# A graph convolution on one core: the order of each engine's work within a block is rewritten, and GpSimd waits per chunk

## The chip, the cores and the metric

The kernel runs on one core of a Trainium2 chip. The metric is the device time of one execution in microseconds (us). Three runs were timed, and one further execution was profiled. The engines are called TensorE (PE; PEld is its weight load), VectorE (DVE), ScalarE (ACT), GpSimd (POOL) and SyncE (SP), as in the profile.

## The reference, cut to what matters

12500 nodes with 128 features, 412500 edges sorted by destination. For each edge a small network of its 8 scalars gives 4 x 32 weights, which multiply the source node's features; four attributes enter as well, and the edges' results are summed by destination.

```python
x0, x1 = node_input[:, :32], node_input[:, 32:].reshape(N, 32, 3)
f0 = x0 @ W1_0e / sqrt(32); f1 = einsum('nui,uw->nwi', x1, W1_1o) / sqrt(32)
feat0, self0 = f0[:, :32], f0[:, 32:]; feat1, self1 = f1[:, :32], f1[:, 32:]
e0, e1 = feat0[edge_src], feat1[edge_src]
h = gelu(edge_scalar_attr @ W_mlp1 / sqrt(8)); h = gelu(h @ W_mlp2 / sqrt(64))
w00, w01, w10, w11 = h @ Wp_00, h @ Wp_01, h @ Wp_10, h @ Wp_11
mid0 = [w00*e0*ea0, w11*sum(e1*ea1)/sqrt(3)]; mid1 = [(w01*e0)*ea1, w10*e1*ea0]
n0, n1 = segment_sum(mid0, edge_dst), segment_sum(mid1, edge_dst)
y = cos(MIX)*self + sin(MIX)*(n @ W2)
out = layernorm(x + y)
```

## The kernel before

A prologue multiplies all nodes by their weights, stores the table of features in DRAM, lays the self part into `acc` (feature by node, in SBUF), and turns the sorted indices into `src_all` and `rel_all` (each destination as an offset from its tile's base). Then come 202 blocks of 2048 edges: 16 tiles of 128 edges, in four chunks of four tiles. An epilogue transposes `acc` and normalises rows.

For each block the engines do the following, each in its own list, and they meet only through semaphores:

- POOL (`gather_block`, L448): 16 indirect gathers (`gather`, L434), each 128 rows of 512 B from the table, into one of four slots of `gath`. Ahead of a block it waits for the indices and for `s_prod[3]` of the block four back, whose slot it takes.
- PE: of the hidden layers, `layer1` (L729) and `layer2` (L733) for two halves h of a later block, all four results in one PSUM bank (`hid_ps`), so they alternate with ACT's gelus; `radial` (L737), the product with `wpbd` for a chunk, into that chunk's bank (2 to 5); `segment_sum` (L750), four matmuls of a chunk with the selection, into bank 6; `transpose_sums` (L764), four transposes of a pair of chunks into bank 7; `convolve` (L773), four matmuls into bank 1 (`y_ps`).
- DVE: `select` (L974) makes the selection (offset equals window position, times the edge's attributes); `products` (L1002) multiplies a chunk's radial weights by gathered rows, three instructions (L994, L997 twice); `add_windows` (L1016) adds 16 windows of 8 nodes into `acc` at bases from registers.
- ACT: `gelu1` (L515), `gelu2` (L520), `lay_attributes` (L526), which copies the attributes into PSUM for DVE, `copy_sums` (L534) of bank 6 to `zsb`, `copy_transposed` (L538) of bank 7 to `ztsb`, `copy_indices` (L500) for the block seven ahead.
- SP loads attributes and scalars in a ring of eight blocks.

A block's work ahead of the loop is called `step`; PE's (L781), DVE's (L1025) and ACT's (L546) set the order by hand, as do the loops of eight steps that follow. One bank for the sums means that a pair of chunks must be copied out by ACT before the next pair is summed, so sums of chunks 2 and 3 of block b-1 stand within step b:

```python
segment_sum(b, s, 0, first)
...
layer1(s, 1)
radial(b, s, 3, first)
segment_sum(b, s, 1)
...
layer2(b + SUPER, 1)
transpose_sums(b, 0, first)
```

## Time and profile before

| what | us |
|---|---|
| median of 3 runs | 5393.78 |
| lowest, highest | 5361.47, 5398.54 |
| the profiled execution | 5384.89 |
| its span, first to last instruction | 5383.0 |
| PE busy | 3296.7 (61% of the span) |
| POOL busy | 3103.5 (58%) |
| DVE, ACT busy | 1881.7 (35%), 1178.5 (22%) |
| granted TensorE clock, mean | 0.767 |

The profile is of a single execution. "Idle before" is an engine's idle time just ahead of an instruction, with what ended it; "remote" is written where no releaser was found, "issue" where the engine waited for nothing that the profile shows. The ends of matmuls are modelled. Register, semaphore and DMA-issuing instructions don't count as busy, except POOL's indirect gathers.

### The profile page before, as it was taken

The numbers are of one execution on the slowest core, as the hardware profiler recorded it, in microseconds if no ns is written. First come the engines' busy times: TensorE is split into PE (matmuls) and PEld (weight loads), VectorE is DVE, ScalarE is ACT, GpSimd is POOL, SyncE is SP. The second block draws the span as 40 slices with busy tenths as digits, with TensorE's granted clock in tenths as the row PEclk, the third lists the DMA queues.
The fourth block names the chain that finished last, engine by engine and source line by source line (L and its number), as shares of the span: only waits on it lengthen the run. The fifth ranks groups of instructions, "written<-read, shape, count | busy, mean of one in ns | idle before, by whom it ended". The sixth has DMA issues, their size and how long they took to land.

```text
span 5383.0 us, 53986 instructions
## 1 busy us (share of the span) xinstructions
PE 3296.7 (61%) x15272; PEld 1820.5 (34%) x15272; DVE 1881.7 (35%) x6401; ACT 1178.5 (22%) x2646; POOL 3103.5 (58%) x3281
## 2 busy tenths in 40 slices
PE   6566655666665665666566555666666665666666
PEld 5333333333333333333333333333333333333334
DVE  2333333333333333333333333333333333333335
ACT  3222122222222221222222222222222222222224
POOL 5466555566655565556655665556565566555651
PEclk8777777777777777777777777777777787778777
DMA  6122112212212122222221221212222122122211
GB/s 152 34 47 46 44 42 44 44 44 47 46 43 46 42 46 44 44 45 45 46 45 43 47 46 42 45 44 46 43 46 45 43 46 46 43 46 45 46 45 60
DMA packets 586055, 256.02 MB, mean 48 GB/s; under 512 B 528383, under 2 KB 531867, under 8 KB 584347
## 3 DMA queue, kind: packets, MB, share of 16 engines
q0 software_dynamic: 103616, 211.52, 15.1%
q1 hardware_dynamic: 480572, 42.82, 6.7%
q14 instruction: 160, 1.31, 0.1%
q10 hardware_dynamic: 1696, 0.18, 0.0%
q8 instruction: 11, 0.18, 0.0%
HBM read 241.45 MB, written 12.81 MB: 47 GB/s over the span
## 4 chain that ended last, share of the span: by engine, by line
another core or an unknown queue 51%; PE 27%; issue 13%; ACT 8%; DVE 0%; ACTq 0%; DMA 0%; DVEq 0%; POOL 0%; POOLq 0%
PE bank L735 6%; PE bank L778 5%; PE bank L730 5%; PE bank L745 5%; PE bank L759 3%; PE bank L770 2%; ACT h L517 2%; ACT big L522 1%; ACT ztsb L543 1%; ACT ztsb L544 1%; PE bank L677 1%; ACT bank L532 1%; ACT idx L501 1%; ACT big L635 1%
## 5 line engine op out<-in xcount | busy, mean ns | idle before, releaser
L436 POOL DMA_INDIRECT gath<-feature_table,idx x3224 | 3077.2, 954 | 2149.6 <-issue 1711.0
L745 PE MATMUL bank<-wpbd,big 128*128 128x256 f32 x3232 | 982.4, 433 | 27.1 <-issue 25.5
L994 DVE TENSOR_TENSOR big<-bank,gath 128x256 f32<-128x256 f32 x808 | 342.2, 424 | 1737.2 <-remote 1481.8
L778 PE MATMUL bank<-ztsb,conv 128*128 128x128 f32 x1616 | 360.4, 392 | 865.4 <-ACT ztsb L544 574.8
L745 PEld LDWEIGHTS bank<-wpbd,big 128*128 128x128 f32 x3232 | 707.5, 225 | 472.5 <-issue 404.1
L997 DVE TENSOR_TENSOR big<-bank,gath 128x384 f32<-128x384 f32 x1616 | 817.9, 548 | 0.0
L770 PE MATMUL bank<-ident,zsb 128*128 128x128 f32 x1616 | 342.8, 351 | 700.3 <-issue 505.4
L735 PE MATMUL bank<-h,w2bd 128*128 128x512 f32 x804 | 571.8, 801 | 232.2 <-ACT h L517 128.0
L1022 DVE TENSOR_TENSOR acc<-acc,bank 128x8 f32 x3232 | 528.7, 164 | 509.4 <-PE bank L778 93.3
L730 PE MATMUL bank<-e8T,w1bd 128*128 128x512 f32 x804 | 571.0, 799 | 156.2 <-ACT big L522 77.6
L778 PEld LDWEIGHTS bank<-ztsb,conv 128*128 128x128 f32 x1616 | 308.1, 285 | 982.5 <-issue 492.6
L759 PE MATMUL bank<-big,sel 128*32 128x256 f32 x6464 | 593.4, 444 | 8.8 <-DVE big L997 8.7
L770 PEld LDWEIGHTS bank<-ident,zsb 128*128 128x128 f32 x1616 | 258.4, 183 | 970.1 <-issue 749.1
L522 ACT ACTIVATE big<-bank 128x512 f32<-128x512 f32 x402 | 440.7, 1096 | 618.4 <-PE bank L735 403.5
L536 ACT COPY zsb<-bank 128x512 f32<-128x512 f32 x404 | 237.9, 589 | 1124.4 <-remote 1033.2
L981 DVE TENSOR_TENSOR sel<-rel_all,bank 128x128 f32<-128x128 f32 (+1 forms) x202 | 58.1, 288 | 1102.1 <-issue 940.4
L517 ACT ACTIVATE h<-bank 128x512 f32<-128x512 f32 x402 | 242.1, 602 | 778.7 <-remote 368.0
L543 ACT COPY ztsb<-bank 128x64 f32<-128x64 f32 x404 | 95.8, 237 | 1440.6 <-remote 1364.8
L730 PEld LDWEIGHTS bank<-e8T,w1bd 128*128 128x128 f32 x804 | 145.7, 227 | 380.2 <-issue 235.3
L735 PEld LDWEIGHTS bank<-h,w2bd 128*128 128x128 f32 x804 | 154.0, 238 | 333.3 <-issue 190.7
L759 PEld LDWEIGHTS bank<-big,sel 128*32 128x32 f32 x6464 | 135.7, 115 | 286.2 <-issue 286.1
L986 DVE TENSOR_TENSOR sel<-sel,bank 128x512 f32<-128x512 f32 x202 | 138.7, 686 | 6.9
(83 smaller groups left out, 799.0 us busy)
## 6 DMA issues: line engine op xcount, KB each, us to landing
gath<-feature_table,idx POOLq DMA_INDIRECT x3224
e<-in_edge_attr SPq DMA_DIRECT2D x416, 32.0 KB
ea_t<-in_edge_attr SPq DMA_DIRECT2D x100, 64.0 KB
feature_table<-gath SPq DMA_DIRECT2D x4, 1280.0 KB, 5.6
out<-big SPq DMA_DIRECT2D x4, 1280.0 KB
big<-in_x SPq DMA_DIRECT2D x3, 1280.0 KB, 8.4
dst_rows<-in_dst SPq DMA_DIRECT2D x1, 1536.0 KB
big<-in_src SPq DMA_DIRECT2D x1, 1408.0 KB
```

The source lines that it names most:

```text
L436: pool.indirect_dma_start(out=gath[:, s % SLOTS, t, :], out_offset=None, in_=table[:, :], in_offset=bass.IndirectOffsetOnAxis(ap=idx[:, s, ...
L517: act.activation(h1[:, h, :], hid_ps[:, :], ACT.Gelu_apprx_tanh, scale=1.0 / math.sqrt(RADIAL)).then_inc(s_h1[h], 1)
L522: act.activation(h2[:, m // SUPER % 2, :, :, 2 * (m % SUPER) + h], hid_ps[:, :].rearrange("q (b p) -> q b p", b=SUPER), ACT.Gelu_apprx_tan ...
L730: pe.matmul(hid_ps[:, :], w1bd[:, 2 * (m % SUPER) + h, :], e8T[:, :], start=True, stop=True)\
L735: pe.matmul(hid_ps[:, :], w2bd[:, :], h1[:, h, :], start=True, stop=True).then_inc(s_h2p[h], 1)
L745: last = pe.matmul(wgt_ps[c][:, 256 * r:256 * (r + 1)], h2[:, s // SUPER % 2, s % SUPER, 16 * g:16 * (g + 1), :].rearrange("q p a -> q (p ...
L759: last = pe.matmul(z_ps[32 * t:32 * (t + 1), c % 2, :], sel[:, s % 2, CT * c + t, :, :].rearrange("q k w -> q (k w)"), prod[:, c, t, :], s ...
L770: last = pe.transpose(zt_ps[:, h, c, :], zsb[:, c, 128 * h:128 * (h + 1)], ident[:, :])
L778: last = pe.matmul(y_ps, conv[:, k, :], ztsb[:, k, :], start=(k == 0), stop=(k == 3))
L994: dve.tensor_tensor(o[:, :, :, 0, :], w[:, :, :, 0, :], f[:, :, 0, :].unsqueeze(2).to_broadcast([128, n, 2, MUL]), ALU.mult)
L997: last = dve.tensor_tensor(o[:, :, h, 1:4, :], w[:, :, h, 1, :].unsqueeze(2).to_broadcast([128, n, 3, MUL]), f[:, :, 1:4, :], ALU.mult)
L1022: dve.tensor_tensor(acc[:, at], acc[:, at], y_ps[:, WINDOW * t:WINDOW * (t + 1)], ALU.add)\
```

## The change

The number of matmuls, products, gathers and additions stays. What changes:

- `step` becomes `cycle` on PE, ACT and DVE, in another order. The hidden layers run for block b+5 and b+6 rather than b+4. Radial products of chunks 0 and 1 are made for block b+2, of 2 and 3 for b+1. All four chunk sums of a block stand in a row, and both pairs are transposed in the next cycle.
- Sums and transposes of pair 0 are in bank 6, of pair 1 in bank 7, in turn; `zsb` holds both pairs.
- Products of chunks 0 and 1 of odd blocks go to another buffer (`prod_odd`, in `dst_rows`), so that these chunks' products may be one block further ahead of the sums.
- POOL waits ahead of every chunk for that chunk's product four blocks back (the argument `b_stop` is not used).
- The attributes and the window positions are read from SBUF (`ea_t`, `iota_w`), and `lay_attributes` is gone; SP waits for the selection instead.

```diff
+        prod_odd = dst_rows[:, 0:2 * CT, :].rearrange("q (c t) f -> q c t f", c=2)
+        def prod_at(s, c):
+            return prod_odd[:, c] if c < 2 and s % 2 else prod[:, c]
...
-        z_ps = bank[6][:, :].rearrange("q (c f) -> q c f", c=2)
-        zt_ps = bank[7][:, :].rearrange("q (h c n) -> q h c n", h=2, c=2)
+        z_ps = [bank[6 + i][:, :].rearrange("q (c f) -> q c f", c=2) for i in range(2)]
+        zt_ps = [bank[6 + i][:, :].rearrange("q (h c n) -> q h c n", h=2, c=2) for i in range(2)]
...
-                    if free is not None:
-                        pool.wait_ge(s_prod[CHUNKS - 1], free)
-                        pool.sem_inc(s_round, 1)
                     for c in chunks:
+                        if free is not None:
+                            pool.wait_ge(s_prod[c], free)
+                            pool.sem_inc(s_round, 1)
                         gather(s, c)
...
+            def cycle(b, s, group):
+                k = s + SUPER + 2
+                if s > -2:
+                    gelu1(b + (SUPER + 1), 1)
+                if s > 0:
+                    copy_sums(b - 1, 0)
+                    copy_sums(b - 1, 1)
+                if s > -2:
+                    gelu2(b + (SUPER + 1), k - 1, 1)
+                if k % SUPER == 0:
+                    copy_e8T(group)
+                gelu1(b + (SUPER + 2), 0)
+                if s > 0:
+                    copy_transposed(b - 1, 0)
+                    copy_transposed(b - 1, 1)
+                gelu2(b + (SUPER + 2), k, 0)
+                if s > 0:
+                    act.wait_ge(s_prod[CHUNKS - 1], b + 0)
+                    copy_indices(b + (RING - 1), (s + RING - 1) % RING).then_inc(s_idx, 1)
...
             def segment_sum(b, s, c):
                 if c == 0:
                     pe.wait_ge(s_sel, b + 1)
+                    if s > 0:
+                        pe.wait_ge(s_zt, b * 2)
...
-                dve.wait_ge(s_eap, b + 1)
                 dve.tensor_tensor(sel01[:, :, :], rel_all[:, ts_].unsqueeze(2).to_broadcast([128, TILES, WINDOW]),
-                                  iota_ps.unsqueeze(1).to_broadcast([128, TILES, WINDOW]),
+                                  iota_w[:, :].unsqueeze(1).to_broadcast([128, TILES, WINDOW]),
                                   ALU.is_equal).then_inc(s_sel0, 1)
                 dve.wait_ge(s_sel0, b + 1)
...
-                                  attr.unsqueeze(3).to_broadcast([128, TILES, 4, WINDOW]), ALU.mult).then_inc(s_sel, 1)
+                                  ea_t[:, s % RING, :, :].unsqueeze(3).to_broadcast([128, TILES, 4, WINDOW]),
+                                  ALU.mult).then_inc(s_sel, 1)
...
-                if not first:
-                    dve.wait_ge(s_seg[c], b)
+                if c < 2 and s > 1:
+                    dve.wait_ge(s_seg[c], b - 1)
+                if c >= 2 and s > 0:
+                    dve.wait_ge(s_seg[c], b + 0)
```

The first `cycle` shown is ACT's. PE's and DVE's are best seen in the order of their instructions. In the rows below a bank's number is PSUM's: bank0 the hidden layers, bank1 the convolution, bank2 to bank5 the radial products of chunks 0 to 3, bank6 and bank7 sums and transposes.

PE before, the middle of a step in the loop: from the transposes of the last block's second pair to the convolution.

```order
L770 MATMUL bank7<-ident,zsb 128x128 [waits transposed_sums_copied,sums_copied]
L770 MATMUL bank7<-ident,zsb 128x128 x3
L754 REGISTER_ALU [waits selection_ready]
L759 MATMUL bank6<-big,sel 32x256 [waits products_ready0,sums_copied]
L759 MATMUL bank6<-big,sel 32x256 x3
L730 MATMUL bank0<-e8T,w1bd 128x512 [waits gelu2_done0]
L745 MATMUL bank5<-wpbd,big 128x256 [waits products_ready3]
L745 MATMUL bank5<-wpbd,big 128x256
L759 MATMUL bank6<-big,sel 32x256 [waits products_ready1]
L759 MATMUL bank6<-big,sel 32x256 x3
L776 REGISTER_ALU [waits window_added15,transposed_sums_copied]
L778 MATMUL bank1<-ztsb,conv 128x128 [waits selection_ready]
```

Sums of chunks 0 and 1 stand apart, with first layer and radial 3 between them, and the four transposes wait for sums copied within the step.

PE of the changed kernel, the first part of a cycle: from the first layer of the half 0 to radial 0 and 1 of a later block.

```order
L722 MATMUL bank0<-e8T,w1bd 128x512 [waits gelu2_done1]
L737 MATMUL bank5<-wpbd,big 128x256 [waits products_ready3]
L737 MATMUL bank5<-wpbd,big 128x256
L759 MATMUL bank6<-ident,zsb 128x128 [waits sums_copied]
L759 MATMUL bank6<-ident,zsb 128x128 x3
L759 MATMUL bank7<-ident,zsb 128x128 x4
L727 MATMUL bank0<-h1,w2bd 128x512 [waits gelu1_done0]
L737 MATMUL bank2<-wpbd,big 128x256 [waits products_ready0]
L737 MATMUL bank2<-wpbd,big 128x256
L737 MATMUL bank3<-wpbd,big 128x256 [waits products_ready1]
L737 MATMUL bank3<-wpbd,big 128x256
```

All eight transposes stand in a row behind one wait, early in the cycle, and the two radial products follow at once.

PE of the changed kernel, the rest of that cycle.

```order
L749 MATMUL bank6<-dst_rows,sel 32x256 [waits products_ready0,transposed_sums_copied,selection_ready]
L749 MATMUL bank6<-dst_rows,sel 32x256 x3
L749 MATMUL bank6<-dst_rows,sel 32x256 [waits products_ready1]
L749 MATMUL bank6<-dst_rows,sel 32x256 x3
L749 MATMUL bank7<-big,sel 32x256 [waits products_ready2]
L749 MATMUL bank7<-big,sel 32x256 x3
L749 MATMUL bank7<-big,sel 32x256 [waits products_ready3]
L749 MATMUL bank7<-big,sel 32x256 x3
L766 MATMUL bank1<-ztsb,conv 128x128 [waits window_added15,transposed_sums_copied]
L766 MATMUL bank1<-ztsb,conv 128x128 x3
L722 MATMUL bank0<-e8T,w1bd 128x512 [waits gelu2_done0]
```

The four sums stand together behind one wait for the transposed sums' copies; before, only two stood between such waits. The first layer's second half closes the cycle.

DVE before, one step from chunk 1's product on (`sel01` and `sel` are the selection, `base_row` the load of the bases).

```order
L994 TENSOR_TENSOR big<-bank3,gath 128x8x32 [waits segments_summed1,gathered2_1,radial_weights_done1]
L997 TENSOR_TENSOR big<-bank3,gath 128x4x96 x2
L980 REGISTER_ALU [waits selection_ready,segments_summed3]
L981 ISA [waits attributes_in_psum]
L981 TENSOR_TENSOR sel01<-rel_all,bank1 128x128
L986 TENSOR_TENSOR sel<-sel01,bank1 128x512 [waits onehot_ready]
L994 TENSOR_TENSOR big<-bank4,gath 128x8x32 [waits segments_summed2,gathered2_2,radial_weights_done2]
L997 TENSOR_TENSOR big<-bank4,gath 128x4x96 x2
L1010 ISA
L1010 TENSOR_LOAD base_row
L994 TENSOR_TENSOR big<-bank5,gath 128x8x32 [waits segments_summed3,gathered2_3,radial_weights_done3]
L997 TENSOR_TENSOR big<-bank5,gath 128x4x96 x2
```

DVE of the changed kernel, one cycle from its start: the products of chunks 2 and 3 (into `big`), then 0 and 1 of the next block (here into `dst_rows`), then the bases; the two instructions of the selection and the 16 additions follow.

```order
L978 TENSOR_TENSOR big<-bank4,gath 128x8x32 [waits segments_summed2]
L981 TENSOR_TENSOR big<-bank4,gath 128x4x96 x2
L978 TENSOR_TENSOR big<-bank5,gath 128x8x32 [waits segments_summed3,gathered2_3,radial_weights_done3]
L981 TENSOR_TENSOR big<-bank5,gath 128x4x96 x2
L987 REGISTER_ALU
L978 TENSOR_TENSOR dst_rows<-bank2,gath 128x8x32 [waits segments_summed0,gathered3_0,radial_weights_done0]
L981 TENSOR_TENSOR dst_rows<-bank2,gath 128x4x96 x2
L978 TENSOR_TENSOR dst_rows<-bank3,gath 128x8x32 [waits segments_summed1,gathered3_1,radial_weights_done1]
L981 TENSOR_TENSOR dst_rows<-bank3,gath 128x4x96 x2
L996 ISA
L996 TENSOR_LOAD base_row
L960 ISA
```

Four products now stand in a row; before, the selection and the load of bases stood between them.

## Rows read from the trace of the kernel before

**Rows 1.** The page: DMA queues, then groups of instructions.
```profile
q0 software_dynamic: 103616, 211.52, 15.1%
...
L436 POOL DMA_INDIRECT gath<-feature_table,idx x3224 | 3077.2, 954 | 2149.6 <-issue 1711.0
...
L994 DVE TENSOR_TENSOR big<-bank,gath 128x256 f32<-128x256 f32 x808 | 342.2, 424 | 1737.2 <-remote 1481.8
...
L981 DVE TENSOR_TENSOR sel<-rel_all,bank 128x128 f32<-128x128 f32 (+1 forms) x202 | 58.1, 288 | 1102.1 <-issue 940.4
...
L986 DVE TENSOR_TENSOR sel<-sel,bank 128x512 f32<-128x512 f32 x202 | 138.7, 686 | 6.9
```

**Rows 2.** Groups by line, POOL alone, 240.9 to 5273.2 us.
```profile
L436 POOL DMA_INDIRECT gath<-feature_table,idx x3120 | 2977.8, 954 | 2055.5 <-issue 1617.3 <-DVE big L997 438.3
```

**Rows 3.** POOL's waits in that stretch: total us, times, longest us.
```profile
POOL gath L436 <- DVE big L997: 438.3, 72, 11.6
```

**Rows 4.** Timeline of one block: start us, us, engine, line, operation [idle before].
```profile
2105.28 0.96 POOL L436 DMA_INDIRECT gath<-feature_table,idx  x1 [5.41 <-issue]
...
2109.00 1.13 PE L730 MATMUL bank<-e8T,w1bd 128*128 128x512 f32 x2
...
2109.96 1.03 PE L745 MATMUL bank<-wpbd,big 128*128 128x256 f32 x4
...
2110.84 0.60 ACT L517 ACTIVATE h<-bank 128x512 f32<-128x512 f32 x1 [2.28 <-PE bank L730]
...
2110.92 0.64 PE L759 MATMUL bank<-big,sel 128*32 128x256 f32 x8
...
2112.45 1.03 PE L745 MATMUL bank<-wpbd,big 128*128 128x256 f32 x4
...
2113.72 0.42 DVE L994 TENSOR_TENSOR big<-bank,gath 128x256 f32<-128x256 f32 x1 [2.05 <-remote]
...
2118.69 0.58 ACT L536 COPY zsb<-bank 128x512 f32<-128x512 f32 x1 [7.25 <-remote]
...
2119.33 1.12 PE L770 MATMUL bank<-ident,zsb 128*128 128x128 f32 x4 [5.85 <-issue]
...
2124.17 0.95 POOL L436 DMA_INDIRECT gath<-feature_table,idx  x1 [0.30 <-issue]
...
2125.05 0.42 DVE L994 TENSOR_TENSOR big<-bank,gath 128x256 f32<-128x256 f32 x1 [3.40 <-remote]
...
2127.87 0.21 ACT L543 COPY ztsb<-bank 128x64 f32<-128x64 f32 x1 [7.37 <-remote]
...
2128.07 0.42 DVE L994 TENSOR_TENSOR big<-bank,gath 128x256 f32<-128x256 f32 x1 [1.67 <-remote]
...
2128.19 0.62 ACT L517 ACTIVATE h<-bank 128x512 f32<-128x512 f32 x1
...
2128.41 1.01 DVE L997 TENSOR_TENSOR big<-bank,gath 128x384 f32<-128x384 f32 x2
...
2130.20 0.95 POOL L436 DMA_INDIRECT gath<-feature_table,idx  x1 [5.08 <-issue]
```

**Rows 5.** DVE's group L916: 97 to 151 us (gathers run), 161 to 178 us (none).
```profile
L916 DVE COPY acc<-bank 128x500 f32<-128x500 f32 x6 | 4.1, 679 | 54.7 <-remote 44.2 <-issue 10.5
...
L916 DVE COPY acc<-bank 128x500 f32<-128x500 f32 x7 | 4.8, 679 | 1.9 <-PE bank L690 1.9
```

**Rows 6.** Timeline, POOL: first gather of block 1.
```profile
91.10 0.95 POOL L436 DMA_INDIRECT gath<-feature_table,idx  x1 [0.30 <-issue]
```

**Rows 7.** POOL's gathers of the steady part, by source line.
```profile
L436 POOL DMA_INDIRECT gath<-feature_table,idx x3120: 949/955/972, 240.9 to 5267.4; - x195
```

**Rows 8.** Timeline, POOL: the first gather that waits for products.
```profile
190.03 0.95 POOL L436 DMA_INDIRECT gath<-feature_table,idx  x1 [38.77 <-issue]
```

**Rows 9.** Timeline: the last gather (POOL), the last additions (DVE).
```profile
5282.10 0.95 POOL L436 DMA_INDIRECT gath<-feature_table,idx  x1 [0.30 <-issue]
...
5328.19 4.58 DVE L1022 TENSOR_TENSOR acc<-acc,bank 128x8 f32 x16 [2.28 <-PE bank L778]
```

More of the change, by code:

```diff
@@ new lines, in cycle @@
+            def cycle(b, s, group, round_):
+                i, k = b + (SUPER + 2), s + SUPER + 2
+                if s > -2:
+                    layer2(b + (SUPER + 1), 1)
+                if s > -2:
+                    radial(b + 1, s + 1, 2)
+                if k % SUPER == 0:
+                    transpose_e8(k % RING, round_, i)
+                    pe.wait_ge(s_e8T, group + 1)
+                else:
+                    pe.wait_ge(s_h2[1], i)
+                layer1(k, 0)
+                if s > -2:
+                    radial(b + 1, s + 1, 3)
+                if s > 0:
+                    transpose_sums(b - 1)
+                layer2(i, 0)
+                radial(b + 2, s + 2, 0)
+                radial(b + 2, s + 2, 1)
+                if s >= 0:
+                    for c in range(CHUNKS):
+                        segment_sum(b, s, c)
+                if s > 0:
+                    convolve(b - 1)
+                pe.wait_ge(s_h2[0], b + (SUPER + 3))
+                layer1(k, 1)
@@ L1023, in add_windows, with cycle @@
                         .then_inc(s_add[t], 1)
[L1025 to L1034 removed]
+            def cycle(b, s, n, skipped=0):
+                if s >= 0:
+                    products(b, s, 2, n * 2 + s // SLOTS)
+                    products(b, s, 3, n * 2 + s // SLOTS)
+                if s >= -1:
+                    products(b + 1, s + 1, 0, n * 2 + (s + 1) // SLOTS - skipped)
+                    products(b + 1, s + 1, 1, n * 2 + (s + 1) // SLOTS - skipped)
+                    base = load_bases(b - 2) if s >= 2 else None
+                    select(b + 1, s + 1, (n + (s + 1) // RING) * 16 + 16)
+                if s >= 2:
+                    add_windows(b - 2, base)
             flag = dve.value_load(flag_i[0:1, 0:1], min_val=0, max_val=NODES)
```

208 lines of the change are left out of this document (67 added, 141 removed).

## The prediction

> **What bounds the kernel now.** First the page's DMA queues and groups of costly instructions: the gathers' queue takes 15.1% of the DMA engines' time, GpSimd (POOL) has 3224 gathers to issue, and the other engines' large idle times end with "remote", a releaser that the profile can't name [rows 1]. No engine or queue is full, so the waits must be read in order of time.
>
> POOL's own group in the steady part comes next [rows 2]: 5032.3 us hold 3120 gathers, 195 blocks of 16, so a block takes 25.81 us. A gather is 0.954 us and the next follows 0.30 us later; 16 x 0.954 + 15 x 0.30 = 19.8 us is a burst. The idle 2055.5 us less 195 x 15 x 0.30 leave 1178 us, 6.0 us per block, in which POOL stands still. 19.8 + 6.0 = 25.8: the period is a burst and a stop, and an edit counts only if it changes one of the two. Stops run up to 11.6 us [rows 3].
>
> The timeline shows what a stop is made of [rows 4]. POOL waits for product 3 of the block four back. Look at when that becomes possible. TensorE (PE) ends the sums of chunk 3 (L759) at 2111.56, and ACT, which waits for just that, starts its copy only at 2118.69, 7.1 us later. The transposes end at 2120.45, and the copy that waits for them starts at 2127.87, 7.4 us later. The radial product of chunk 2 ends at 2113.48, and VectorE (DVE) begins on it at 2125.05. DVE doesn't wait for gathered rows there: POOL has issued them three blocks before. At the start of the burst it is not so: the first layer ends at 2110.13 and its gelu starts at 2110.84. After the last gather (ends 2125.12) all that is outstanding is let go: copy 2127.87, product 2128.07, gelu 2128.19. So while POOL issues, a finished matmul is seen late by whoever waits, and it comes out at the latest 2.75 us after the last gather. That this belongs to the gathers the prologue shows: the same copy L916, fed by the same matmuls, idles 54.7 us before 6 copies while POOL gathers, and 1.9 us before 7 when it doesn't [rows 5]. I call the release behind a burst the flush.
>
> Of the Trainium skill, "SBUF — State Buffer", section "SBUF: two separate sides", this speaks against: engine ports and DMA ports can't contend, and PE and ACT never wait on anyone. [Rows 4, 5] show waits on PE that depend on POOL's gathers; the measurement decides, and the sum stands on it.
>
> The stop, step by step [rows 4]: 2.75 us to the flush, 0.2 us to the start of DVE's product (2127.87 to 2128.07), 1.35 us for its three instructions (to 2129.42), 0.78 us to POOL's first gather at 2130.20: 5.08 us. The mean is 6.0, so 0.96 us per block is lateness: blocks in which PE still had a dependent step to do when POOL stopped, here the chain sums 3, copy, transposes, copy, and first layer, gelu, second layer, gelu, first layer, all ahead of radial product 3 in PE's list.
>
> **The change, part by part.**
> POOL's waits. Four waits on a register value per block in place of one, and each is met by a product of its own chunk. The next burst starts at chunk 2 (product 2 of the new VectorE cycle comes first) and runs over c2, c3, c0, c1, since the four products then follow each other at 1.35 us while four gathers take 5.0. I expect again 16 gathers between two stops. Cost of three more waits: nothing to 0.3 us (another issue gap) each in a burst; in the prologue the second block's first gather also stands behind a wait (for its indices), and follows in the usual 0.30 us [rows 6], so I take nothing. The index copy that POOL also waits for stays at the end of ACT's list and runs seven blocks ahead; SP's loads wait for the selection instead of the attribute copy, and load as many blocks ahead as before.
>
> PE's list. No matmul is added or removed. In a cycle PE now does the second layer, radial 2, first layer, radial 3, eight transposes, second layer, radial 0 and 1, four sums, convolution, first layer. The radial products that DVE needs behind the next flush are all done early in the burst. What must be seen within a burst before the sums can run is the first layer (gelu) and the transposes (their copies hold the sums' banks); the long pair sums-copy-transposes has its first half at the flush, where it is free. In [rows 4] the first layer (ends 2110.13, 4.9 us into the burst) is seen 0.7 us later, radial 1 (ends 2110.99, 5.7 us) 2.7 us later, sums 3 (6.3 us) 7.1 us later. The new transposes end about 6 us into the burst: after the flush gelu 0.6, second layer 1.1, gelu 1.1, first layer 1.1, radial 1.0, transposes 1.1 and issue in between make some 8 us, and the burst starts 2.1 us behind the flush. Seen 2.7 to 7.1 us later, copied in 0.5 to 1 us, and followed by four sums at 0.64 us and the loads between them, the sums end 12 to 18 us into a burst of 19.8. So PE mostly has nothing left that DVE needs when POOL stops.
> New stop: 2.75 + 0.3 (sums 0 and 1 and others stand ahead of sums 2 in the release; in [rows 4] copy, product and gelu come out over 0.3 us) + 1.35 + 0.78 = 5.18 us. Of the 0.96 us of lateness I leave 0.36: 5.54 us. Bounds: 5.1, the shown stop, and 11.6, the longest; the value lies between the shown one and today's mean, the rows nearest to it. Gain 0.50 us per block.
>
> The second bank for the sums and the doubled products of chunks 0 and 1 only make this order possible: copies and products are as many and as long as before. ACT's copy of attributes (L532) goes; ACT idles 7.25 and 7.37 us before its two copies [rows 4], so nothing.
>
> DVE's selection. Both instructions, 0.288 and 0.686 us [rows 1], now read two operands from SBUF, where the second used to be in PSUM. They fall into the burst, 5.4 us behind the flush. The trace has no such instruction beside a gather. Bounds: nothing, or POOL held for both, 0.98 us per block; less than nothing is excluded, since POOL doesn't wait for them. DVE itself has the time (idle 1737 us before L994, [rows 1]). I take 0.2 us, nearer to nothing, because gathers keep 949 to 972 ns beside all that DVE does now [rows 7].
> The same page and section of the Trainium skill has a rule here: a DVE instruction with two SBUF inputs and a GpSimd one that reads SBUF lock each other out for the whole instruction. By it the upper bound would hold; it is a rival below.
>
> Ends. The first gather that waits starts at 190.03 [rows 8], behind product 3 of block 0. It will wait for product 0 only, about 5 us earlier. From the last gather's end (5283.05) to the end of the last additions (5332.77) four blocks take 49.7 us, 12.4 each [rows 9]. The additions now come a block later and the hidden layers are two blocks ahead instead of fewer, so about one block more: +12 us. Together +7.
>
> Sum: 198 blocks x (-0.50 + 0.20) = -59, +7: -52 us. From the profiled execution, 5384.9 us (span 5383.0 and 1.9 around it), that is 5333. The median of the three runs is 8.9 above the profiled one, so I forecast 5342 us, 1.0% under 5393.8.
>
> **Rivals.**
> Nothing changes. The flush is what POOL waits for, both lists need one, and 6.0 us remain. For it: the stop shown is already 5.08, within 0.1 of the new floor. Against it: the mean is 0.96 above. 5393.8 + 7 = 5401, "same".
>
> The selection holds POOL (other side). If both instructions stop the gathers, +0.98 in place of +0.20: 198 x 0.78 = +154, so 5496. It decides against the change from 0.5 us per block on. For it: select now falls always into a burst. Against it: no row shows POOL held by DVE.
>
> The sums come too late (other side). They now need the transposes of the same burst to be seen and copied, behind PE's in-order list. If these are seen only at the flush, their copies and four sums at 0.64 us or more follow while POOL stands, and a stop is 5 us longer, like those of up to 11.6 us [rows 3, 4]. Ten more such stops eat up the gain of 52; in 40 of 198 blocks it is +200: 5540.
>
> POOL gets past a chunk. If product 2 is released within the burst, 20 gathers run per stop in place of 16; the stop of 5.5 us is then spread over 1.25 blocks, -1.1 us per block: 5342 - 218 = 5124. Against it: eleven results stand ahead of sums 2, and [rows 4] show one release in 5 to 6 us there (2113.72, 2118.69, 2125.05).
>
> **Chances and range.** Forecast case (stop 5.2 to 5.8, selection up to 0.4) 0.50, between 5240 and 5400: 0.32 of it faster, 0.18 same. Nothing changes 0.12. Selection holds POOL 0.13 (0.09 slower, 0.04 same). Late sums 0.15 (0.13 slower, 0.02 same). Past a chunk 0.10. Faster by over 1% 0.42, within 1% 0.36, slower by over 1% 0.22; 1% is about what a measurement of this kernel tells from no change (its three runs lie 0.7% apart). Lower end: stop at its floor of 5.18 and selection free give 198 x -0.86 + 7 = -163, so 5230. Upper end: 5496, the selection's price. I give 5230 to 5500.
>
> **What would show it.** POOL's group: idle per block (now 6.0 beside the 4.5 of issue gaps) should fall to 5.5, with bursts still 16 gathers, beginning at chunk 2. A gather of 1.2 us and more, or gaps over 0.30 beside the selection rows, would show the lock. If ACT's copies of transposes or PE's sums appear in the stops, the list is late. If bursts of 20 or no stops appear, the delay isn't what I take it for and the forecast is far too high; two stops per block would put it at 30 us a block.

## The result, and the profile after

The changed kernel takes 5424.75 us (median of 17 runs, 5416.69 to 5431.13) beside 5392.95 us of the kernel before (17 runs). The ratio on record is 1.0054, with a 95% interval from 1.0036 to 1.0071. It is slower by 0.5%: within the 1% that the prediction called "same" and inside its 5230 to 5500 us, but on the other side of no change from the 1.0% faster that it gave as its number. The profiled execution has a span of 5429.1 us, 46.1 more than before; the medians differ by 32.

The first view is POOL again, in the same stretch as [rows 2, 3]: its group, then its waits (total us, times, longest us).

```profile
L439 POOL DMA_INDIRECT gath<-feature_table,idx x3098 | 2959.9, 955 | 2072.6 <-DVE big L981 1170.9 <-issue 901.7
```

```profile
POOL gath L439 <- DVE big L981: 1170.9, 194, 9.0
POOL gath L439 <- issue: 901.7, 2904, 0.9
```

A gather is as long as before. The pattern stands as forecast: 194 stops with 16 gathers between two of them, all behind DVE's product, and nothing but issue gaps elsewhere. 1170.9 / 194 is 6.04 us per stop, where 5.5 were forecast. Before it was 5.88: the 195 stops of [rows 2], counted one by one in the timeline, sum to 1146.9 us. (The prediction's 6.0 came from taking 0.30 us for every issue gap; they are 0.311 on the mean, before and after.) The longest stop is 9.0 us in place of 11.6. So the stops were not shortened; their mean grew by 0.16 us.

The mean hides the cause. POOL's idle times before the first gather of each burst, read one by one over the two traces and sorted by whether ACT copied fresh scalars (`e8T`) in that block, give this table. Every fourth block has such a copy, because the scalars of four blocks are transposed together.

| mean stop, us | before | after |
|---|---|---|
| 49 blocks with a copy of `e8T` | 6.80 | 7.88 |
| 146 other blocks | 5.57 | 5.41 |
| stops under 5.4, of 196 | 74 | 100 |
| stops of 6.5 and more, of 196 | 22 | 57, 48 of them with `e8T` |

49 x 1.08 - 146 x 0.16 = +30 us. Three blocks in four gained 0.16 us each, the fourth gave it back and more. These blocks were already the longer ones before, by 1.2 us; now it is 2.5. What those blocks wait for has rows of its own. First the groups of the kernel before, in the stretch of [rows 2]: PE's transposes of the scalars and ACT's copy of them.

```profile
L699 PE MATMUL bank<-ident,e 128*128 128x128 f32 x196 | 31.8, 288 | 0.0
...
L513 ACT COPY e8T<-bank 128x512 f32<-128x512 f32 x49 | 28.7, 585 | 87.8 <-PE bank L699 54.6 <-issue 33.3
```

The same two groups of the changed kernel:

```profile
L691 PE MATMUL bank<-ident,e 128*128 128x128 f32 x196 | 53.3, 427 | 363.3 <-DMA e<-in_edge_attr 301.7 <-issue 61.6
...
L516 ACT COPY e8T<-bank 128x512 f32<-128x512 f32 x49 | 28.7, 586 | 412.8 <-PE bank L691 270.6 <-issue 142.2
```

PE never waited for scalars before. Now it stands still for them 363.3 us, 7.4 per time, and what ends most of the wait is the transfer of the scalars (`e`). Their transposes began 3.2 us into a burst on the mean before, and 11.8 now (10.8 to 13.6 in the 49 blocks). The timeline of one such block shows what follows (start us, us, engine, line, operation):

```profile
2640.58 0.95 POOL L439 DMA_INDIRECT gath<-feature_table,idx  x1 [5.22 <-DVE big L981]
...
2642.88 1.07 ACT L532 COPY zsb<-bank 128x512 f32<-128x512 f32 x2
...
2643.10 0.95 POOL L439 DMA_INDIRECT gath<-feature_table,idx  x1 [0.30 <-issue]
...
2643.81 0.69 DVE L969 TENSOR_TENSOR sel<-sel,ea_t 128x512 f32<-128x512 f32 x1
...
2644.36 0.97 POOL L439 DMA_INDIRECT gath<-feature_table,idx  x1 [0.30 <-issue]
2644.68 0.39 SPq L345 DMA_DIRECT2D ea_t<-in_edge_attr  x1
2645.25 6.36 SPq L316 DMA_DIRECT2D e<-in_edge_attr  x4
...
2651.60 1.09 PE L691 MATMUL bank<-ident,e 128*128 128x128 f32 x4 [6.58 <-DMA e<-in_edge_attr]
...
2652.73 0.59 ACT L516 COPY e8T<-bank 128x512 f32<-128x512 f32 x1 [7.44 <-PE bank L691]
...
2653.37 2.07 PE L722 MATMUL bank<-e8T,w1bd 128*128 128x512 f32 x2 [0.68 <-issue]
...
2656.94 1.91 PE L759 MATMUL bank<-ident,zsb 128*128 128x128 f32 x8
...
2659.48 0.96 POOL L439 DMA_INDIRECT gath<-feature_table,idx  x1 [0.30 <-issue]
...
2662.14 0.21 ACT L539 COPY ztsb<-bank 128x64 f32<-128x64 f32 x1 [6.07 <-remote]
...
2663.58 0.21 ACT L539 COPY ztsb<-bank 128x64 f32<-128x64 f32 x1 [1.00 <-remote]
...
2664.07 1.93 PE L749 MATMUL bank<-big,sel 128*32 128x256 f32 x32 [2.59 <-ACT ztsb L540]
...
2665.74 0.42 DVE L978 TENSOR_TENSOR big<-bank,gath 128x256 f32<-128x256 f32 x1 [16.39 <-PE bank L749]
...
2667.87 0.95 POOL L439 DMA_INDIRECT gath<-feature_table,idx  x1 [7.43 <-DVE big L981]
```

Read it from the selection (2643.81) on. As soon as it ends, SP issues a load of attributes and then four of scalars, in the order of its list. PE has been standing at the transposes of just those scalars. They arrive at 2651.60, 11 us into the burst, and behind them in PE's list stand the first layer, a radial product and the eight transposes of sums. These end at 2658.85, their copies start only at 2662.14, when POOL has stopped, and the sums run in the stop. That is a stop of 7.43 us. The first gather that waits for products, and the last gather, hold the rest of the 46.1 us:

```profile
187.68 0.96 POOL L439 DMA_INDIRECT gath<-feature_table,idx  x1 [36.66 <-issue]
...
5312.33 0.96 POOL L439 DMA_INDIRECT gath<-feature_table,idx  x1 [0.30 <-issue]
```

From the last gather's end to the end of the span are 115.8 us; before they were 100.0 (from [rows 9] and the span). The first gather that waits starts 2.35 us earlier (187.68 for 190.03 in [rows 8]). -2.35 + 15.8, and +32.6 between these two points, are the 46.1; the +30 of the stops is nearly all of the 32.6.

### The profile page after: what moved, and what is told of

It reads as the page before. It is cut to its first block, busy times and chain, and to the rows that moved or that the text cites. A ratio compares the mean times of both kernels' runs of the same rounds, so it can differ in the third digit from the quotient of the medians.

```text
span 5429.1 us, 53623 instructions
## 1 busy us (share of the span) xinstructions
PE 3437.7 (63%) x15318; PEld 1905.2 (35%) x15318; DVE 1813.9 (33%) x6409; ACT 1173.1 (22%) x2455; POOL 3106.7 (57%) x3281
## 4 chain that ended last, share of the span: by engine, by line
issue 64%; PE 11%; SPq 10%; another core or an unknown queue 8%; DVE 4%; ACT 2%; DVEq 1%; DMA 0%; ACTq 0%; POOL 0%; POOLq 0%
SPq L316 8%; PE bank L749 3%; PE bank L722 2%; PE bank L737 2%; PE bank L727 1%; PE bank L766 1%; DVE big L981 1%; DVE acc L1008 1%; SPq L345 1%; PE bank L669 1%; ACT big L627 1%; DVE dst_rows L981 1%; SPq L366 1%; PE bank L759 0%
## 5 line engine op out<-in xcount | busy, mean ns | idle before, releaser
L749 PE MATMUL bank<-big,sel 128*32 128x256 f32 x4848 | 834.3, 509 | 1029.4 <-issue 830.0
L978 DVE TENSOR_TENSOR big<-bank,gath 128x256 f32<-128x256 f32 x608 | 252.9, 416 | 3040.6 <-remote 1811.2
L737 PE MATMUL bank<-wpbd,big 128*128 128x256 f32 x3256 | 867.2, 402 | 0.0
L749 PEld LDWEIGHTS bank<-big,sel 128*32 128x32 f32 x4848 | 251.0, 131 | 1524.4 <-issue 1286.8
L981 DVE TENSOR_TENSOR big<-bank,gath 128x384 f32<-128x384 f32 x1216 | 613.9, 545 | 0.0
L727 PE MATMUL bank<-h,w2bd 128*128 128x512 f32 x814 | 464.8, 654 | 142.6 <-ACT h L520 139.1
L691 PE MATMUL bank<-ident,e 128*128 128x128 f32 x208 | 55.3, 420 | 366.4 <-DMA e<-in_edge_attr 301.7
L749 PE MATMUL bank<-dst_rows,sel 128*32 128x256 f32 x1616 | 130.5, 448 | 216.5 <-issue 157.7
L759 PE MATMUL bank<-ident,zsb 128*128 128x128 f32 x1616 | 229.6, 289 | 0.0
L759 PEld LDWEIGHTS bank<-ident,zsb 128*128 128x128 f32 x1616 | 211.0, 152 | 29.0 <-issue 8.7
```

What stands on the lines that cost most here:

```text
L727: pe.matmul(hid_ps[:, :], w2bd[:, :], h1[:, h, :], start=True, stop=True).then_inc(s_h2p[h], 1)
L737: last = pe.matmul(wgt_ps[c][:, 256 * r:256 * (r + 1)], h2[:, s // SUPER % 2, s % SUPER, 16 * g:16 * (g + 1), :].rearrange("q p a -> q (p ...
L749: last = pe.matmul(z_ps[c // 2][32 * t:32 * (t + 1), c % 2, :], sel[:, s % 2, CT * c + t, :, :].rearrange("q k w -> q (k w)"), prod_at(s, ...
L759: last = pe.transpose(zt_ps[pair][:, h, c, :], zsb[:, pair, c, 128 * h:128 * (h + 1)], ident[:, :])
L978: dve.tensor_tensor(o[:, :, :, 0, :], w[:, :, :, 0, :], f[:, :, 0, :].unsqueeze(2).to_broadcast([128, n, 2, MUL]), ALU.mult)
L981: last = dve.tensor_tensor(o[:, :, h, 1:4, :], w[:, :, h, 1, :].unsqueeze(2).to_broadcast([128, n, 3, MUL]), f[:, :, 1:4, :], ALU.mult)
```

## The experiments

The runs were made in ten sets, each on one chip, with the kernel before beside them. **The pace goes with the chip.** In two sets (e7 and e8; e16), on two chips, the kernel before took 5396 us, near the 5393 of this case, whose own chip isn't on record. In the eight others, on six chips, it took 4197 to 4206 us. I call the first the pace with stops, the second the quick pace. No chip showed both; one of the quick ones was used in three sets. Both kernels show the same instructions at both. This is e2's trace at the quick pace (the kernel before with POOL's waits per chunk): POOL's group from 240.9 to 4000 us, then the copy of [rows 5] from 97 to 151 us, while gathers run, then sums and ACT's copy of them.

```profile
L436 POOL DMA_INDIRECT gath<-feature_table,idx x2984 | 2850.3, 955 | 908.9 <-issue 906.2 <-ACT idx L501 2.7
```

```profile
L916 DVE COPY acc<-bank 128x500 f32<-128x500 f32 x9 | 6.1, 679 | 3.0 <-PE bank L690 3.0
```

```profile
2109.29 0.64 PE L759 MATMUL bank<-big,sel 128*32 128x256 f32 x8 [1.64 <-DVE big L997]
2110.00 0.59 ACT L536 COPY zsb<-bank 128x512 f32<-128x512 f32 x1 [2.57 <-PE bank L759]
```

908.9 / 2984 is 0.30 us: POOL never stops, and a gather every 1.26 us is the pace of the kernel. The sums end at 2109.93 and ACT sees them 0.07 us later, while POOL gathers just as in [rows 4], where it took 7.1. The copy idles 3.0 us before 9, where [rows 5] have 54.7 before 6. So the late sight of PE's results while POOL gathers is found on some chips, not on all. What differs between these chips isn't in a trace.

**e1: POOL waits once per block again.**

```diff
-                    for c in chunks:
-                        if free is not None:
-                            pool.wait_ge(s_prod[c], free)
+                    if free is not None:
+                        pool.wait_ge(s_prod[CHUNKS - 1], free)
+                    for c in chunks:
```

> The changed kernel, but POOL waits once per block for product 3 four blocks back, as before the change. My theory (a burst of 16 gathers, then a stop that lasts from the last gather over the release of PE's results to the first product that POOL waits for): POOL now waits for the second product behind the release, not for the first, so each stop grows by one product, 1.26 us, to 7.3 us: 198 x 1.26 = +250, about 5675 us. Rival (what a stop costs is PE's lateness, and POOL's wait point does not matter): within 20 us of 5425.

4226.8 us, ratio 1.0071 (1.0055 to 1.0088), at the quick pace. POOL waits for nothing there, so this says nothing on the stops. The changed kernel itself was never met at the quick pace; its distance from the kernel before is read from this variant and the ones below. PE's transposes of scalars in e1, over the stretch of [rows 2]:

```profile
L691 PE MATMUL bank<-ident,e 128*128 128x128 f32 x192 | 51.7, 424 | 823.5 <-DMA e<-in_edge_attr 431.3 <-issue 391.8 <-ACT big L526 0.4
```

PE stands still for 17 us before them here, in 48 blocks, and POOL never stops. So late scalars don't make a stop by themselves; they do where the results that come after them are seen late too.

**e2: the kernel before, with POOL's waits per chunk** (the reverse of e1's edit).

> The kernel before, with POOL's waits per chunk alone. If a stop is set by the one product that comes last behind the release, the burst only begins at another chunk and nothing changes: 5375 to 5410 us, bursts of 16. If the waits per chunk carry a gain of their own, because chunks 0 to 2 are released within the burst, POOL starts up to 1.3 us per block earlier: down to 5135. If they cost something, it is three waits per block, up to 0.3 us each: up to 5570.

4198.0 us, 1.0001 (0.9991 to 1.0011), quick pace. Three more waits per block cost nothing measurable where they are met. What they do in stops wasn't seen.

**e3: the kernel before, its selection reading SBUF.**

```diff
-                                  iota_ps.unsqueeze(1).to_broadcast([128, TILES, WINDOW]),
+                                  iota_w[:, :].unsqueeze(1).to_broadcast([128, TILES, WINDOW]),
...
-                attr = ea_ps.rearrange("q (t k) -> q t k", k=4)
+                attr = ea_t[:, s % RING, :, :]
```

> The kernel before, but the two instructions of the selection read window positions and attributes from SBUF as in the changed kernel (ACT's copy into PSUM stays, and is read by nobody). If both operands in SBUF hold POOL up for the instruction, +0.98 us per block, up to 5585 us; my estimate in the prediction was +0.2, 5433; if there is no such cost, 5380 to 5405.

4201.7 us, 1.0010 (1.0001 to 1.0020), quick pace: about 4 us, 0.02 per block. 21 gathers are longer than 0.985 us, with 4.0 us of excess together, 19 of them begun under the multiplication L986. So two operands in SBUF can hold POOL, but it depends on where the gathers begin; e8 and e14 settle that.

**e4, e9, e11, e12, e15, e16: the transposes of sums ahead of radial 2 and 3.** One kernel on six occasions.

```diff
-                if s > -2:
-                    radial(b + 1, s + 1, 2)
                 if k % SUPER == 0:
...
                 layer1(k, 0)
-                if s > -2:
-                    radial(b + 1, s + 1, 3)
                 if s > 0:
                     transpose_sums(b - 1)
+                if s > -2:
+                    radial(b + 1, s + 1, 2)
+                    radial(b + 1, s + 1, 3)
```

> The changed kernel, with PE's radial products of chunks 2 and 3 moved behind the eight transposes (the same work, another order). In its trace a quarter of the stops last 7.2 us and more, and in these the copies of the transposes start only when the gathers have ended. Count theory (while POOL gathers, PE's instructions are seen as done one after the other, about one per gather, so what matters is how many stand ahead of the result that is waited for): 8 fewer instructions stand ahead of the copies, they come about 8 gathers or 10 us earlier, the late stops go, and the mean stop falls from 6.04 to 5.2 or 5.3: about 5425 - 198 x 0.8 = 5265 us. Rival (each result is seen late by a time of its own, wherever it stands): no change, 5415 to 5435.

> The kernel of e4 again (PE's radial products 2 and 3 behind the eight transposes), for the pace with stops. Count theory (while POOL gathers, PE's instructions are seen as done one after the other, about one per gather): 8 fewer instructions ahead of the transposes' copies, these are seen 8 to 10 us earlier, the late stops (7.2 us and more, a quarter of them) go, the mean stop falls from 6.0 to 5.2: 5265 us, ratio 0.976. Rival (each result is seen late by a time of its own): 5415 to 5435. At the pace without stops: 4226 to 4236, ratio 1.007.

> The kernel of e4 and e9 (PE's radial products 2 and 3 behind the eight transposes), once more for the pace with stops, which needs a chip that shows it (the expectation is that of e9): count theory 5265 us, ratio 0.976, mean stop 5.2 us in place of 6.0, no stops over 7 us; rival (each result is seen late by a time of its own) 5415 to 5435, ratio 1.005. At the pace without stops 1.007.

> The kernel of e4, e9 and e11 (PE's radial products 2 and 3 behind the eight transposes), once more for the pace with stops. Count theory 5265 us, ratio 0.976, mean stop 5.2 us in place of 6.0, no stops over 7 us; rival (each result is seen late by a time of its own) 5415 to 5435, ratio 1.005. At the pace without stops 1.007 to 1.009.

> The kernel of e4 (PE's radial products 2 and 3 behind the eight transposes). At the pace with stops: count theory 5265 us, ratio 0.976, mean stop 5.2 us in place of 6.0, no stops over 7 us; rival (each result is seen late by a time of its own) 5415 to 5435, ratio 1.005. At the pace without stops 1.007 to 1.009.

> As e15: at the pace with stops count theory 5265 us, ratio 0.976, mean stop 5.2 us and none over 7 us; rival 5415 to 5435, ratio 1.005. At the pace without stops 1.007 to 1.009.

The first five met the quick pace: 1.0078, 1.0076, 1.0087, 1.0076 and 1.0082, as the changed kernel's other variants. e16 met the stops: 5384.9 us, ratio 0.9986 (0.9960 to 1.0012), beside 1.0051 (1.0022 to 1.0080) of e7. The order gives 0.65% back, some 35 us, not the 160 of the count theory, and more than the 0 of its rival. POOL's waits of e16, in the stretch of [rows 3]:

```profile
POOL gath L439 <- DVE big L980: 1116.2, 195, 8.1
```

5.72 us per stop. The same sorting as above says where: the blocks with `e8T` fall from 7.80 (e7) to 6.58, the others stay (5.38 and 5.43). One of the former:

```profile
2618.19 0.38 SPq L345 DMA_DIRECT2D ea_t<-in_edge_attr  x1
2618.75 5.65 SPq L316 DMA_DIRECT2D e<-in_edge_attr  x4
...
2624.99 1.09 PE L691 MATMUL bank<-ident,e 128*128 128x128 f32 x4 [7.44 <-DMA e<-in_edge_attr]
...
2629.72 0.21 ACT L539 COPY ztsb<-bank 128x64 f32<-128x64 f32 x1 [0.26 <-issue]
...
2635.65 0.21 ACT L539 COPY ztsb<-bank 128x64 f32<-128x64 f32 x1 [5.50 <-remote]
...
2636.14 2.38 PE L749 MATMUL bank<-big,sel 128*32 128x256 f32 x32 [0.45 <-ACT ztsb L540]
...
2640.36 0.96 POOL L439 DMA_INDIRECT gath<-feature_table,idx  x1 [6.37 <-DVE big L980]
```

PE still waits for scalars, as long as in the changed kernel. Only what comes after is shorter: radial 3 no longer stands between the scalars and the transposes of sums (radial 2 was done before the wait in the changed kernel, so it is 4 instructions fewer there, not 8). On the mean of these blocks the first copy of transposed sums starts 16.3 us into the burst in place of 21.8 (e7), the last one 21.9 in place of 23.3. So what stands ahead of a result matters where the result was going to be late. e16's ratio can't be told from 1: it takes the loss back and isn't faster than the kernel before.

**e5, e10: fewer semaphore updates by PE** (radial 0 and 1 share one, both pairs of transposes share one, sums 0 have none; the waits follow). One of the five places:

```diff
-                last.then_inc(s_w[c], 1)
+                if c % 2 == 1:
+                    last.then_inc(s_w[c], 1)
```

> The changed kernel with 11 instead of 15 semaphore updates by PE per block (radial products 0 and 1 give one between them, the two pairs of transposes one, sums 0 none), the same matmuls in the same order. The kernel before has run at two paces so far, 5393 us (POOL stands still for 6 us per block) and 4197 us (POOL issues a gather every 1.26 us without a stop). At the first pace: if each semaphore update of PE is held back for about 5 us while POOL gathers (update theory), one fewer stands ahead of the copies of transposes, 5 us earlier, and the late stops go: down to 5265 us. If it is the instructions that are held back (count theory), nothing changes: 5415 to 5435 us. At the second pace both say 4225 to 4230 us.

> The kernel of e5 again (11 instead of 15 semaphore updates by PE per block, the same matmuls), for the pace with stops. Update theory (each update is held back by about 5 us while POOL gathers): down to 5265 us. Count theory (it is the instructions that are held back): 5415 to 5435. At the pace without stops: 4226 to 4236.

1.0074 and 1.0073, both at the quick pace. The two theories are not told apart by it.

**e13: more matmuls ahead of the transposes** (`for r in (0, 1, 0, 1, 0, 1) if c == 2 else (0, 1)` in `radial`).

> The changed kernel, but PE makes each radial product of chunk 2 three times over (the same matmul into the same place, 8 more PE instructions of 0.25 us per block, ahead of the transposes). At the pace with stops: count theory, 8 more instructions stand ahead of the transposes' results, these are seen 8 to 10 us later, which is behind the burst in most blocks: stops of 7.3 us and more in place of 6.0 on the mean, 198 x 1.5 = +300, 5725 us, ratio 1.06. Rival (each result is seen late by a time of its own, whatever stands ahead): only the 2 us of PE's own work are added, and these lie within the burst: 5425 to 5470, ratio up to 1.014. At the pace without stops PE has idle time enough: 4226 to 4240, ratio 1.007 to 1.01.

1.0081 (1.0059 to 1.0104), quick pace: 2 us more of PE's work per block cost at most a few us in all, PE has room there. The stops weren't met.

**e6: product 2 in two halves, POOL waits for the first half** ahead of two gathers.

> The changed kernel, but DVE makes product 2 in two halves, and POOL waits for the first half alone ahead of two gathers. At the pace of 5393 us, where POOL stands still until product 2 is there behind the release: POOL starts 0.6 us earlier in each block, 198 x 0.6 = 119, so 5306 us (stops of 4.5 instead of 5.1 us). If the stop is not set by this product, 5425. At the pace of 4197 us, where POOL never waits, 4225 to 4230 us.

1.0074 (1.0045 to 1.0104), quick pace. It says nothing on the stops.

**e7: the changed kernel once more.**

> The changed kernel as it is, next to the kernel before. Six runs of its variants stood at the quick pace (POOL never waits) and all came out at 1.0071 to 1.0078 times the kernel before, whatever they changed in POOL's waits or PE's order. If at that pace only the ends and the length of the gathers count, the kernel itself gives 1.0075 too, with a mean gather of 0.960 us and 77 us from the last gather to the end. At the slow pace (stops of 6 us) it must give 1.0054 again.

It met the stops: 5425.9 us, 1.0051 (1.0022 to 1.0080), 1164.0 us in 194 waits of POOL. So the case's result comes again in a set of its own. (The variants of the changed kernel run before it were four, e1, e4, e5 and e6, not six.)

**e8, e14: the selection's first result in PSUM.** The multiplication then has one operand in SBUF and not two. Since the bank is shared with the convolution, DVE also waits for it ahead of the selection, and PE for the selection once, so "nothing else moves" isn't quite so.

```diff
-                dve.tensor_tensor(sel01[:, :, :], rel_all[:, ts_].unsqueeze(2).to_broadcast([128, TILES, WINDOW]),
+                dve.tensor_tensor(sel01_ps, rel_all[:, ts_].unsqueeze(2).to_broadcast([128, TILES, WINDOW]),
...
-                dve.tensor_tensor(sel[:, s % 2], sel01[:, :, :].unsqueeze(2).to_broadcast([128, TILES, 4, WINDOW]),
+                dve.tensor_tensor(sel[:, s % 2], sel01_ps.unsqueeze(2).to_broadcast([128, TILES, 4, WINDOW]),
```

> The changed kernel, but the first instruction of the selection writes its result to PSUM and the second reads it there, so that the multiplication (0.69 us) has one operand in SBUF and not two; nothing else moves. Lock theory: a gather that begins while a DVE instruction with two SBUF operands runs is held until that one ends; in the run with one wait per block 85 gathers are longer than 0.985 us and their excess is 17.8 us. Here no gather is, the mean falls from 0.960 to 0.955 us, and the time by 16 to 18 us at the quick pace: about 4209 for 4227, ratio 1.003 to 1.004. Rival (the long gathers come from SP's loads or from DVE's additions, which run beside them too): the mean stays 0.960 and the time 4227. At the slow pace the selection is not beside a gather's beginning, and both say no change.

> The kernel of e8 again (the multiplication of the selection has one operand in SBUF and one in PSUM), now for the pace without stops. Lock theory: no gather over 0.985 us behind the prologue, mean gather 0.955 in place of 0.960 us, 16 to 18 us less than the changed kernel's variants at that pace: ratio 1.003 to 1.004 in place of 1.007 to 1.008. Rival (the long gathers come from SP's loads or DVE's additions): 1.007 to 1.008. At the pace with stops 1.0055, as in e8.

With stops (e8): 5432.9 us, 1.0055 (1.0032 to 1.0079), the same as e7 within the intervals. At the quick pace (e14): 4208.4 us, 1.0025 (1.0012 to 1.0039), beside 1.0082 (1.0052 to 1.0111) of e15 in the same set; e1, e4 and e12 without the edit have 1.0071 to 1.0078. Both halves of the lock theory came out in the time. The gathers of e1 (quick pace, selection from SBUF), by their shortest, median and longest ns:

```profile
L439 POOL DMA_INDIRECT gath<-feature_table,idx x2974: 951/955/1457, 239.1 to 3999.7; - x199
```

and one of its long ones, behind one of usual length:

```profile
508.07 0.95 POOL L439 DMA_INDIRECT gath<-feature_table,idx  x1 [0.30 <-issue]
508.70 0.29 DVE L965 TENSOR_TENSOR sel<-rel_all,iota_w 128x128 f32<-128x128 bf16 x1 [0.56 <-issue]
509.03 0.69 DVE L969 TENSOR_TENSOR sel<-sel,ea_t 128x512 f32<-128x512 f32 x1
...
509.33 1.22 POOL L439 DMA_INDIRECT gath<-feature_table,idx  x1 [0.30 <-issue]
```

The gather begins 0.30 us into the multiplication, 0.39 before its end, and is 0.26 us longer than usual. It is so throughout: of the 72 gathers of e1 that begin with 0.17 us or more of the multiplication to come, 69 are longer by what is left of it less 0.12 to 0.13 us; the other three begin within 0.03 us of its start and are of usual length. All 85 gathers over 0.985 us hold 17.8 us of excess. e14's gathers, same view, whose longest excess is a tenth of a us:

```profile
L439 POOL DMA_INDIRECT gath<-feature_table,idx x2979: 954/958/1049, 240.1 to 3999.0; - x199
```

There 132 gathers begin with as much of the multiplication to come, and none of them is longer than the median by more than 0.002 us. So it is the operand, not the added waits. (The median is 958 and not 955 ns, and the profiled execution took 4217.4 us, the longest of e14's six, so the forecast mean of 0.955 was not seen.)

At the pace with stops the burst begins with the release, so the selection stands at a fixed place in it: it starts 3.2 us into the burst in the block shown above (2643.81 for 2640.58) and ends 0.14 us behind the start of the fourth gather (2644.36), which takes 0.97 us. In that trace 170 gathers begin under the multiplication, with at most 0.15 us of it to come, and none is longer by more than 0.03 us. That is why the two operands in SBUF cost some 18 us at one pace and nothing at the other.

**e17, e18: e16's, e6's and e8's edits together.**

> The changed kernel with the edits of e16, e6 and e8 together (transposes ahead of radial 2 and 3; product 2 in halves, POOL waits for the first half; the selection's first result in PSUM). At the pace with stops: e16 gave 5385; the release no longer has a whole product behind it but a half, 0.6 us less per stop (mean 5.7 to 5.1): 5385 - 198 x 0.6 = 5265 us, ratio 0.976. If POOL's start isn't set by that product, 5385. At the pace without stops: 4208 as in e14, ratio 1.003, since only the selection counts there.

> The kernel of e17 again, for the pace with stops: 5265 us, ratio 0.976, mean stop 5.1 us in place of 5.7, if half a product stands where a whole one stood between the release and POOL's start; 5385 if not. At the pace without stops 1.003.

1.0029 (1.0016 to 1.0042) and 1.0031 (1.0016 to 1.0047), quick pace twice: e14's gain is kept, the stops weren't met. No version here beats the kernel before at either pace.

## Why the prediction was wrong, step by step

**What bounds the kernel** was right for the pace of this case: bursts of 16 gathers, a stop whose end is one of DVE's products behind the release, and a shortest usual stop of 5.18 us (the median of the ordinary blocks is 5.19 after the change; 100 of 196 stops lie under 5.4, in e7 as well). Its lateness was mis-sized: the mean stop before was 5.88, so 0.80 us above the shown 5.08 and not 0.96. With that alone the forecast would have been 198 x (5.54 - 5.88 + 0.20) + 7 = -21 us in place of -52: 0.4% faster, within "same", and still on the wrong side. e2's trace qualifies one sentence of it: that a finished matmul is seen late while POOL gathers doesn't follow from these instructions alone, since the same ones show no lateness on other chips. Nor do [rows 4, 5] speak against what the prediction cites of the Trainium skill, which is about ports of SBUF: they show results seen late, and no row shows a port as the reason.

**POOL's waits** priced at nothing: right at the quick pace (e2), and at the pace with stops the gaps inside the bursts are 0.311 us on the mean before and after. e2's kernel didn't meet the stops.

**PE's list.** The new stop was to be 5.18 + 0.36 = 5.54 us. In three blocks of four it is 5.41, a little better than that. In the fourth it is 7.88. "The new transposes end about 6 us into the burst" is near in an ordinary block (7.2 us on the mean of 145) and is 18 us in the others (2658.85 for a burst from 2640.58 in the block shown). "The sums end 12 to 18 us into a burst" holds in neither: in ordinary blocks they begin 13.3 us into it and the last ends at 22.9, in 134 of 145 behind the end of the last gather, because PE starts its matmuls one by one there (the lines are in the last section). In the blocks with `e8T` they begin only at 23.6 and end at 26.2. So "PE mostly has nothing left that DVE needs when POOL stops" was wrong everywhere, and that the ordinary stop came out near its number owes something to luck: there most of the sums had run, and the product that POOL waits for began 3.1 us (median) behind the last gather, where 3.05 were forecast.

**The step that failed** is the clause on SP: "SP's loads wait for the selection instead of the attribute copy, and load as many blocks ahead as before". The loads do, but their reader doesn't: PE now transposes scalars from block b+6 on where it did from b+4 on. The last of the four blocks' scalars are loaded when the selection of block b+1 is done (`sp.wait_ge(s_sel, ...)`), and DVE makes that one in the same cycle b, some 4 us into the burst; six more go by in loading. The lead that hid the load was used up by the two blocks, and I had priced the move at nothing without asking what was next to be late. It costs 1.08 us in 49 blocks, 53 us, and the 0.16 us gained in the others bring 23. That the load is the cause is argued from the traces (0 us of waiting for scalars before, 363.3 after, a stop that is long just there) and not shown by an experiment: a kernel with the scalars loaded earlier wasn't tried. e16 shows the other half: with the load as late, but radial 3 no longer behind it, the stop is 1.2 us shorter in these blocks alone.

**DVE's selection**, taken at 0.20 us of 0 to 0.98: it is nothing at this pace (e7 and e8). The rule of the Trainium skill, "SBUF — State Buffer", section "SBUF: two separate sides", is that a DVE instruction with two SBUF inputs and a GpSimd one that reads SBUF lock each other out. The runs agree in one direction: e1 and e14 show gathers held by the multiplication, at some 18 us in 4227. In the other direction they don't: 162 multiplications of e1 begin under a running gather and take 0.69 to 0.72 us, no longer than usual. The upper bound would need a gather to begin near the start of the multiplication in every block; the row of gathers from 949 to 972 ns told nothing of it, because its kernel had no such instruction.

**The ends**, +12 and -5, sum +7: measured +15.8 and -2.35, sum +13. At the quick pace the end alone is +11.6 (76.9 us from the start of the last gather to the end in e1, 65.3 in e2), which is the block that was counted; with the 17.8 us of long gathers it accounts for nearly all of e1's 29.5 us there.

**The rivals.** "Nothing changes" (5401) is nearest in number. "The sums come too late" is what happened in a block of four, at 2.5 us over the rest (of which 1.2 were there before) and not 5, and with a cause that it didn't name.

## What to carry to other kernels

When a change makes a stage work further ahead, its inputs have to move ahead by as much: for every load, write down the block that it brings, the wait that it stands behind and the block that its reader now asks for. A mean over blocks hides a period; sort the stops by what only some blocks do (here one in four) before an average goes into a sum. And where a mechanism has no cause that the kernel explains, see whether another chip shows it before a schedule is built on it.

## What the runs showed of the hardware that was not expected

- The same program runs at 5396 us on two chips and at 4197 to 4206 us on six others. The gathers are as long (955 ns) and as far apart (0.30 us); the difference is that at the slower pace results of PE are seen up to 11.6 us late while POOL issues gathers (radial 2 of [rows 4]), and 0.07 us after their end in e2's trace. Why isn't known.
- At the pace with stops it isn't only the sight of results that is late. In an ordinary block of the changed kernel PE starts its matmuls one at a time inside the burst, 1.4 us apart, though the profile shows nothing that they wait for ("issue"). The burst runs from 2615.49 to 2635.37:

```profile
2615.49 0.95 POOL L439 DMA_INDIRECT gath<-feature_table,idx  x1 [5.60 <-DVE big L981]
...
2622.55 1.04 PE L759 MATMUL bank<-ident,zsb 128*128 128x128 f32 x8
...
2630.12 1.07 PE L749 MATMUL bank<-dst_rows,sel 128*32 128x256 f32 x16 [3.95 <-issue]
...
2631.01 0.61 PE L749 MATMUL bank<-big,sel 128*32 128x256 f32 x7
2632.43 0.38 PE L749 MATMUL bank<-big,sel 128*32 128x256 f32 x1 [0.82 <-issue]
2633.83 0.38 PE L749 MATMUL bank<-big,sel 128*32 128x256 f32 x1 [1.02 <-issue]
...
2634.41 0.96 POOL L439 DMA_INDIRECT gath<-feature_table,idx  x1 [0.30 <-issue]
...
2635.23 0.59 PE L749 MATMUL bank<-big,sel 128*32 128x256 f32 x1 [1.03 <-issue]
```

 That is near one per gather (1.26 us). Whether the two belong together isn't shown: e13, made to test it, met only the quick pace.
- At the quick pace a gather that begins under a DVE multiplication with both operands in SBUF is longer by what is left of the multiplication less 0.13 us (69 gathers of e1); one that has begun before isn't touched (at the other pace, the gather of 2643.10 takes 0.95 us, though the multiplication starts at 2643.81).
